# A selective scan over PSUM in two pieces instead of three, with TensorE's and ScalarE's orders rewritten around it

## The reference, cut to what matters

```
h  = softmax(x x^T / 16) x                      # within each segment of 128 rows
xz = layernorm(h) W_in^T ;  x_in, z = split(xz) # 2 x 512 wide
u  = silu(conv4(x_in) + b) ;  dt = softplus(u W_dt^T + b_dt)
B, C = u W_B^T, u W_C^T                         # 16 states
h_t = exp(dt_t A) h_(t-1) + dt_t B_t u_t        # for each of 512 channels x 16 states
y_t = sum over states of h_t C_t ;  h += (y silu(z)) W_out^T
h  += 64 experts, 8 chosen of 4 groups, capacity 256, on layernorm(h)
```

## Time and profile before

| | us |
|---|---|
| median of three runs | 3821.16 |
| lowest and highest | 3820.72, 3831.04 |
| the profiled execution, its own time | 3815.21 |
| its span, first to last instruction | 3813.3 |

### The profile page before, as it was taken

One profiled execution on the slowest core, in us unless ns is written; L12 is line 12 of the kernel. 1 busy time (PEld: TensorE's weight loads), 2 busy tenths in 40 slices (PEclk: granted clock), 3 DMA queues, 4 the chain that ended last, 5 costly groups with the idle time before them and its releaser, 6 DMA issues. The chain is left out here.

```text
span 3813.3 us, 65702 instructions
## 1 busy us (share of the span) xinstructions
PE 3190.2 (84%) x19681; PEld 2528.9 (66%) x19681; DVE 3016.4 (79%) x5267; ACT 2879.0 (75%) x5580; POOL 2106.1 (55%) x780
## 2 busy tenths in 40 slices
PE   5898898988888888888888898898898888566664
PEld 3777776776777677777777777676677667445453
DVE  3888888888888888888888888888888898544442
ACT  4998988888888888888888888888888888121110
POOL 0555555555555555555555555555555556157776
PEclk8999999999999999999999999999999998678887
DMA  2111111111111111111111111111111111157775
GB/s 84 47 47 55 55 43 56 57 57 55 51 53 40 56 57 57 57 57 52 54 57 57 57 55 43 57 57 57 49 56 52 40 52 50 42 135 146 147 151 86
DMA packets 175733, 241.57 MB, mean 63 GB/s; under 512 B 32816, under 2 KB 154128, under 8 KB 175376
## 3 DMA queue, kind: packets, MB, share of 16 engines
q1 hardware_dynamic: 150800, 199.44, 16.3%
q0 software_dynamic: 24576, 37.77, 6.0%
HBM read 176.07 MB, written 61.08 MB: 62 GB/s over the span
## 5 line engine op out<-in xcount | busy, mean ns | idle before, releaser
L345 POOL TENSOR_TENSOR hid<-hid,c_all 128x1536 f32<-128x1536 f32 x512 | 1771.0, 3459 | 1491.6 <-DVEq L563 1489.6
L568 DVE TENSOR_TENSOR_SCAN hid<-decay,hid,psB 128x512 f32<-128x512 f32 x1024 | 1310.7, 1280 | 119.3 <-PE psB L826 12.4
L826 PE MATMUL psB<-ident,dbu_t 128*128 128x128 f32 x6144 | 936.7, 285 | 236.8 <-DVE hid L568 224.0
L363 ACT ACTIVATE dbu_t<-dtu_t,b_t 128x512 f32<-128x512 f32 x1536 | 995.5, 714 | 159.8 <-PE psB L826 158.2
L375 ACT ACTIVATE decay<-dt,a_neg 128x383 f32<-128x383 f32 x2048 | 1085.8, 606 | 0.0
L826 PEld LDWEIGHTS psB<-ident,dbu_t 128*128 128x128 f32 x6144 | 721.8, 145 | 446.6 <-DVE hid L568 325.7
L838 PE MATMUL psY<-ident,hid 128*128 128x128 f32 x6144 | 780.7, 278 | 33.1 <-POOL hid L345 32.3
L838 PEld LDWEIGHTS psY<-ident,hid 128*128 128x128 f32 x6144 | 714.2, 145 | 77.6 <-POOL hid L345 34.4
L568 DVE TENSOR_TENSOR_SCAN hid<-decay,psB 128x512 f32<-128x512 f32 x512 | 624.0, 1219 | 103.4 <-PE psB L826 72.0
L898 PE MATMUL psM<-u,w_dt 128*128 128x384 f32 x1024 | 354.7, 489 | 18.3 <-ACT turned L384 14.7
L898 PEld LDWEIGHTS psM<-u,w_dt 128*128 128x128 f32 x1024 | 184.4, 190 | 127.8 <-ACT turned L384 21.3
(11 more groups left out here) (148 smaller groups left out, 3520.4 us busy)
## 6 DMA issues: line engine op xcount, KB each, us to landing
c_all<-bc_rows_dram SPq DMA_DIRECT2D x128, 768.0 KB, 4.9
out_dram<-h SPq DMA_DIRECT2D x64, 384.0 KB, 3.5
h<-out_dram SPq DMA_DIRECT2D x32, 384.0 KB, 3.4
x_weights_dram<-normed SPq DMA_DIRECT2D x32, 384.0 KB, 2.5
xs<-in_x_dram SPq DMA_DIRECT2D x32, 256.0 KB
e_wg<-in_gate_dram SPq DMA_DIRECT2D x64, 128.0 KB
e_wu<-in_up_dram SPq DMA_DIRECT2D x64, 128.0 KB
e_wd<-in_down_dram SPq DMA_DIRECT2D x64, 128.0 KB
```

Of the source, the lines that this page charges most:

```text
L345: nc.gpsimd.tensor_tensor(hid[k % 4][:, :, :], hid[k % 4][:, :, :], c_all[:, k, :].unsqueeze(1).to_broadcast([P, CH, L]), ALU.mult).then_i ...
L363: last = nc.scalar.activation(dbu_t[k % 2][:, t, :], dtu_t[q][:, t, :], ACT.Copy, scale=b_t[q][:, t, k:k + 1])
L568: nc.vector.tensor_tensor_scan(h[:, lo:hi], flat(decay[k % 4])[:, lo:hi], psB[:, j, :], h[:, lo - 1:lo] if j else 0.0, ALU.mult, ALU.add). ...
L826: last = nc.tensor.transpose(psB[:, j, i * P:(i + 1) * P], dbu_t[k % 2][:, t, c * P:(c + 1) * P], ident[:, :])
```

## The change

The scan of a step is made in two pieces, of 1024 and of 512 columns; `psB` still has three banks, and `turn_dbu` fills two banks (eight transposes) and then one (four). In TensorE's step `turn_dbu` 0 comes first, then `sum_y`, then `turn_dbu` 1, and all the step's products stand behind it. In ScalarE's step `first_rstd` comes first (that of sequence b-2 in step 1, no longer 2), then `scaled_dbu`, then all copies, with `softplus` among them, and `decays` nearly last. On VectorE both `drive`s are in step 11, behind `attended`; three waits of the routing move from behind their instruction to the head of the function that needs it. The transposed rows DU0 and DU1 are both made in step 12.

```diff
-PB = 3
+PIECES = ((0, 2), (2, 3))
+PB = len(PIECES)
...
-        psB = ps("psB", [P, PB, 512])
+        psB = ps("psB", [P, NSEG, 512])
...
@@ ScalarE's body
-                    if front:
-                        if k == 0:
-                            copy_turned("XN0", b, 0)
-                        if k in (1, 2):
-                            copy_xin(b, 2 * k - 2)
-                        if k in (5, 6, 7, 8):
-                            biased_dt(b, k - 5)
-                        if k in (12, 13):
-                            copy_dtu(b, r, 2 * (k - 12))
-                    if late and k == 9:
-                        copy_turned("X2T1", b, 1)
-
+                    if late and k == 1:
+                        first_rstd(o, 1)
+                    if early and k == 13:
+                        first_rstd(a, 0)
                     if of:
                         scaled_dbu(*of)
                     if front:
                         if k == 0:
+                            copy_turned("XN0", b, 0)
                             copy_turned("XN1", b, 1)
                         if k in (1, 2):
+                            copy_xin(b, 2 * k - 2)
                             copy_xin(b, 2 * k - 1)
...
+                        if k in (5, 6, 7, 8):
+                            biased_dt(b, k - 5)
+                        if k == 8:
+                            softplus(n, b, 1)
+                        if k == 12:
+                            copy_dtu(b, r, 0)
+                            copy_dtu(b, r, 1)
+                        if k == 13:
+                            copy_dtu(b, r, 2)
+                    if late and k == 9:
+                        copy_turned("X2T1", b, 1)
...
                     if late and k == 7:
                         copy_turned("X2T0", b, 0)
+                    if front and k == 7:
+                        softplus(n, b, 0)
                     if early and k == 8:
                         copy_prob_t(b)
-                    if front:
-                        if k == 9:
-                            copy_bc(n, b, r)
-                        if k == 12:
-                            copy_dtu(b, r, 1)
+                    if front and k == 9:
+                        copy_bc(n, b, r)
...
                     if of:
                         decays(*of)
-                    if late and k == 2:
-                        first_rstd(o, 1)
-                    if front:
-                        if k == 3:
-                            after(act, s_yz, n - 1)
-                            silu_z(b, r, 0)
-                            silu_z(b, r, 1)
-                        if k in (7, 8):
-                            softplus(n, b, k - 7)
-                    if early and k == 13:
-                        first_rstd(a, 0)
+                    if front and k == 3:
+                        after(act, s_yz, n - 1)
+                        silu_z(b, r, 0)
+                        silu_z(b, r, 1)
...
@@ VectorE
-                lo, hi = 512 * j, 512 * (j + 1)
+                lo, hi = 512 * PIECES[j][0], 512 * PIECES[j][1]
                 h = flat(hid[k % 4])
-                nc.vector.tensor_tensor_scan(h[:, lo:hi], flat(decay[k % 4])[:, lo:hi], psB[:, j, :],
+                nc.vector.tensor_tensor_scan(h[:, lo:hi], flat(decay[k % 4])[:, lo:hi], flat(psB)[:, lo:hi],
                                              h[:, lo - 1:lo] if j else 0.0, ALU.mult, ALU.add).then_inc(s_h, 1)
...
-                def step(ins, carried=False):
+                def step(ins, last=False):
                     done[0] += 1
                     ins.then_inc(s_rt, 1)
-                    dve.wait_ge(s_rt, ROUTE_STEPS * m + done[0])
-                    if carried:
-                        dve.sem_inc(s_turn, 1)
+                    if not last:
+                        dve.wait_ge(s_rt, ROUTE_STEPS * m + done[0])
...
-                step(nc.vector.tensor_tensor(flat(gsum), v[0], v[3], ALU.add), carried=True)
+                step(nc.vector.tensor_tensor(flat(gsum), v[0], v[3], ALU.add), last=True)
...
             def route_experts(m, step, done):
 
+                dve.wait_ge(s_rt, ROUTE_STEPS * m + done[0])
+                dve.sem_inc(s_turn, 1)
...
-                step(last, carried=True)
+                step(last, last=True)
...
             def weigh(m):
 
+                dve.wait_ge(s_rt, ROUTE_STEPS * (m + 1))
+                dve.sem_inc(s_turn, 1)
...
-                        if k in (10, 11):
-                            drive(n, b, r, k - 10)
+                    if early and k == 11:
+                        attended(a, b)
+                    if front and k == 11:
+                        drive(n, b, r, 0)
+                        drive(n, b, r, 1)
                     if early:
-                        if k == 11:
-                            attended(a, b)
...
@@ TensorE
-                for i in range(4):
-                    c, t = divmod(4 * j + i, NSEG)
-                    last = nc.tensor.transpose(psB[:, j, i * P:(i + 1) * P], dbu_t[k % 2][:, t, c * P:(c + 1) * P],
-                                               ident[:, :])
+                for i in range(4 * PIECES[j][0], 4 * PIECES[j][1]):
+                    c, t = divmod(i, NSEG)
+                    last = nc.tensor.transpose(flat(psB)[:, i * P:(i + 1) * P],
+                                               dbu_t[k % 2][:, t, c * P:(c + 1) * P], ident[:, :])
...
                 for k in range(NS):
+                    if scans:
+                        turn_dbu(b, k, 0)
                     if scans and k >= 3:
                         sum_y(b, k - 3)
                     if back and k < 3:
                         sum_y(m, k + NS - 3)
                     if scans:
-                        turn_dbu(b, k, 0)
                         turn_dbu(b, k, 1)
...
-                    if scans:
-                        turn_dbu(b, k, 2)
-
```

More of the change, by code:

```diff
@@ L718, in route_experts @@
                 step(last)
-                step(nc.vector.memset(gtop[:, :, TOPG:G], ABSENT), carried=True)
+                step(nc.vector.memset(gtop[:, :, TOPG:G], ABSENT))
+                dve.sem_inc(s_turn, 1)
                 for s in range(NSEG):
@@ L726, in route_experts @@
                     out=by_group(masked), in0=flat(gleft).unsqueeze(2).to_broadcast([P, NSEG * G, GE]), scalar=FAR,
-                    in1=by_group(biased), op0=ALU.mult, op1=ALU.add), carried=True)
+                    in1=by_group(biased), op0=ALU.mult, op1=ALU.add))
+                dve.sem_inc(s_turn, 1)
                 for s in range(NSEG):
                     last = nc.vector.max(top8[:, s, :], masked[:, s, :])
-                step(last, carried=True)
+                step(last, last=True)
                 assert done[0] == ROUTE_STEPS
             def weigh(m):
+                dve.wait_ge(s_rt, ROUTE_STEPS * (m + 1))
+                dve.sem_inc(s_turn, 1)
                 for s in range(NSEG):
@@ L964, in body @@
                             turn_normed("XN", b, 0, normed1)
+                            turn_normed("XN", b, 1, normed1)
                         if k in (1, 2):
                             project_xin(b, 2 * k - 2)
+                            project_xin(b, 2 * k - 1)
                         if k == 3:
                             project_z(b, 0)
-                        if k in (5, 6, 7, 8):
-                            project_dt(n, b, k - 5)
-                        if k in (12, 13):
-                            turn_dtu(n, b, 2 * (k - 12))
-                    if late and k == 9:
-                        turn_normed("X2T", b, 1, normed2)
-                    if early and k == 10:
-                        attend(b, 0)
-                    if back and k == 14:
-                        project_out(b, 0)
-                    if scans:
-                        turn_dbu(b, k, 2)
-                    if front:
-                        if k == 0:
-                            turn_normed("XN", b, 1, normed1)
-                        if k in (1, 2):
-                            project_xin(b, 2 * k - 1)
-                        if k == 3:
                             project_z(b, 1)
@@ L991, in body @@
                             project_z(b, 2)
+                        if k in (5, 6, 7, 8):
+                            project_dt(n, b, k - 5)
                     if early:
@@ L998, in body @@
                             scores(b)
-                    if late and k == 7:
-                        pe.wait_ge(s_xn[1], o + 1)
-                        turn_normed("X2T", b, 0, normed2)
-                    if early:
                         if k == 8:
@@ L1005, in body @@
                             turn("PT", b, [prob[:, s, :] for s in range(NSEG)])
-                    if front and k == 9:
-                        project_bc(b)
-                    if early and k == 10:
-                        attend(b, 1)
+                        if k == 10:
+                            attend(b, 0)
```

(23 more changed lines are left out.)

4 lines of the change are left out of this document (2 added, 2 removed).

## The result

| | before | changed |
|---|---|---|
| median of eight runs, us | 3818.11 | 3832.53 |
| lowest and highest | 3814.03, 3831.04 | 3827.13, 3841.73 |
| the profiled execution | 3815.21 | 3831.40 |
| its span | 3813.3 | 3829.2 |
| granted clock, mean | 0.940 | 0.937 |

The ratio is 1.0035, with a 95% interval of 1.002 to 1.0049: the changed kernel is slower, by about 13 us. That lies inside the range of the prediction (3770 to 3870) and 11 us above its point, but it is a change where none was forecast. All times here are of executions in the faster of the device's two states; one of the ten of e7_three took 8946 us, where the other nine took 3809 to 3820, and is left out.

The account below looks back on a forecast made before the run. VectorE was taken to bound most steps, TensorE steps 4 to 10, ScalarE's late instructions before step 14. (-1.04 + 1.25 for the clock) x 30 blocks gave +6, the last blocks -6: forecast 3821 us, range 3770 to 3870.

Parts of the forecast that it names:

- The cost of one scan: VectorE's scan in each step: large piece 2.29 us, fixed cost 0.15, whole scan 3.60, which is 0.31 less.
- T0 to T4: From the first scan piece's start in step 0 to that in step 4: -0.26 us per block, including +1.33 gate wait.
- T4 to T10: From scan start in step 4 to that in step 10, TensorE the chain: 37.4 against 36.92 us, +0.48 per block.
- T10 to T0: From scan start in step 10 to the next block's step 0: -0.95 us up to step 15, then -0.31.
- T15 to T0: From scan start in step 15 to that in the next block's step 0: -0.31 us per block.
- T13 to T15: From scan start in step 13 to that in step 15: 11.52 us, set by TensorE's O0, O1 and transposes.
- The clock: TensorE's clock falling ahead of the gate (about 1.5 us) and step 12 (about 1.0), half the blocks: +1.25 per block.
- The ends: The last two blocks, having little beside their scans, were to give back about 6 us.
- All four: Rival forecasts: clock holds, 3784 us (0.30); slower clock, 3859 (0.20); scan's fixed cost stays, 3868 (0.07); VectorE's whole gain, about 3510 (0.05).
- Rival 2: Clock falls in nearly every block ahead of the gate and of step 12: slower, 3859 us, chance 0.20.
- Rival 4: VectorE's whole gain arrives, 9.6 us per block: about 3510 us, chance 0.05.
- no change: Main forecast for the whole kernel: 3821 us, within 0.3% (11 us) of the kernel before, chance 0.38.

Follow-up runs that it names:

- e7_three: Changed kernel with the scan in three pieces of one bank each, keeping the new orders: 3814.7 us, ratio 0.9982.
- e1_gate: Changed kernel with the sum ahead of turn_dbu 0 in step 2 alone: 3770.4 us, ratio 0.9873.
- f1_smallfirst: Changed kernel with the small scan piece first (512 columns, then 1024): 3755.4 us, ratio 0.9833.
- e3_probt: Changed kernel with ScalarE's copy of PT ahead of softplus 1 again: 3804.8 us, ratio 0.9961.
- e4_rstd: Kernel before with first_rstd at the head of ScalarE's steps 1 and 13, nothing else changed: 3797.6 us, ratio 0.9942.
- e8_filler: Changed kernel with twelve unread transposes in TensorE's idle time ahead of turn_dbu 0 of step 2: 3840.3 us, ratio 1.006.
- e2_pieces: Kernel before with the scan in two pieces and nothing else changed: 3785.1 us, ratio 0.9914.
- g1_spread: Kernel before with the scan in two pieces, plus CB's wide products cut and laid between its narrow ones: 3759.4 us, ratio 0.9854.
- f2_small_probt: Changed kernel with 512 columns first, then 1024, and ScalarE's copy of PT ahead of softplus 1: 3710.3 us, ratio 0.9714.

## Why the prediction was right or wrong

**The cost of one scan: right.** 2285 ns was measured for 1024 columns against 2.29 us, and from 1219 at 512 that is 2.08 ns per column and 0.15 fixed. The Trainium skill ("DVE: opcode table, instruction layouts, handler registers and perf-mode slots", section 6, Feedback) says that the built-in scan runs at half throughput. The trace agrees: 2.08 ns per column against the 1.02 per element that the prediction found for ordinary operations.

**T0 to T4: right in mechanism and size.** The gate waits for the sum behind the large piece; 4.90 against 4.93. e1_gate and f1_smallfirst remove the cause in two different ways, and both times the wait is gone. The wait behind `gsum` was worth about 0.3: T0 to T1 went from 8.53 to 7.90, of which 0.31 are the scan's.

**T4 to T10: right, slightly small.** Where the clock holds it is 37.5 against the 37.4 of the forecast. The two causes named were both there: D2 late by 1.8, and CB's wait for PT, of which e3_probt gave back 1.0.

**T10 to T0: right.** The wait for `rs` is gone, O0 and O1 take its place. T15 to T0 fell by 0.19 in blocks without the jump, where 0.31 was forecast. T13 to T15 is 11.29 where the clock holds, against 11.52 worked out, and e4_rstd shows the same limit in the old order (11.08).

**The clock: right in kind, wrong in its shares.** Half the blocks were taken at both places. It was 16 of 26 ahead of the gate, at 1.4 us each on the mean (0.87 per block, 0.75 taken), and 6 of 26 ahead of or in step 12, at 1.1 (0.26, 0.5 taken). At a third place nothing was taken: behind CB, 8 of 26 blocks have a slow T9 to T10 where the kernel before had 4. The mean T4 to T10 is 0.45 over its shortest, where it was 0.24: +0.2 us per block, 5 us in all. At the two places that were named the clock cost 1.13 us per block, a little less than the 1.25 taken. That the idle time is what costs the clock ahead of the gate is shown by e8_filler. The step that failed here is "The clock", which priced falls at two places only: the trace of before already had T9 to T10 at 9.98 in three blocks instead of 8.33, and I did not ask what made them so. On the rule of the Trainium skill ("TensorE: Matmul & The Clock Gate", section "HAM oscillation — how this bites in real kernels"), that only idle gaps longer than these harm, the trace disagrees: 2.47 us of idle time were followed by the half level.

**The ends: wrong, and this is the larger miss.** The step "the last two blocks, which have little beside their scans, give back about 6" has the wrong sign. The last block's T1 to T2, with nothing to do but gate and scan, went from 5.80 to 8.89, as GpSimd's starts show:

```profile
3205.63 3.44 POOL L349 TENSOR_TENSOR hid<-hid,c_all 128x1536 f32<-128x1536 f32 x1 [4.24 <-DVEq L561]
3214.52 3.44 POOL L349 TENSOR_TENSOR hid<-hid,c_all 128x1536 f32<-128x1536 f32 x1 [5.45 <-DVEq L561]
```

```profile
3212.53 1.89 DVE L576 TENSOR_TENSOR yz_t<-psY,zs_t 128x512 f32<-128x512 f32 x3 [3.30 <-PE psY L842]
```

The gate waits there 3.3 us, at the half level, and nothing hides it; the last two blocks together take 3.6 us more, not 6 less. Adding up the two profiled executions: the 26 blocks +10.1, the blocks ahead of them +3.8 and behind them +2.7, the first scan 4.4 later, the rest of the program 5.1 less: +15.9 us, the difference of the spans. The sum of the prediction, +6 and -6, was right for the middle to 5 us and left out 11 at the ends, where I took the scan's gain and forgot that the gate's wait is there too. A second term was put at nothing, the start. Ahead of the first scan the changed order puts both `drive`s behind `attended`, and the transposes DU wait for them:

```profile
79.23 2.46 PE L851 MATMUL psM<-ident,u 128*128 128x128 f32 x12 [3.15 <-DVE u L672]
```

They begin at 74.63 in the kernel before. The first start of GpSimd is at 84.5 to 87.2 us in the four kernels with the old place of `drive` (before, e2_pieces, e4_rstd, g1_spread) and at 88.8 to 93.0 in the ten with the new one; no edit moved the `drive`s alone. The 5.1 us less at the other end are probably not the change's: e2_pieces and e4_rstd, whose edits are small, have 5.3 and 4.7 less there too.

**The rivals.** All four fell. Rival 2 (slower by the clock, 3859) has the right sign for the wrong reason: it was said to decide above some 55% of the blocks, and 62% fell ahead of the gate, but only 23% at its other place, and the two together cost less than the forecast had taken. What made the kernel slower than the forecast is the third place and the ends. Rival 4's sum comes to about 3527 with the 30 blocks of the others, not 3510, which changes nothing. The forecast of "no change" was a balance of a gain and a loss of nearly equal size, each of which could be off by more than the 11 us of the band.

**Where the expected gain went.** VectorE has 103 us less to do. The order of TensorE gave most of it back: a wait for two thirds of the scan at the head of each step, with the sum behind it. Undoing that in one step of sixteen gives 62 us, splitting the banks the other way 77.

## What to carry to other kernels

When two pieces of work are merged, ask what waits for the first of them, and what stands behind that waiting instruction in its queue; the small piece first keeps the merge's gain and frees the buffer early. Put an instruction that can run at once ahead of one that must wait, step by step, and not by one order for all: here the sum belongs first in the steps where TensorE waits, the transposes in those where TensorE is late. A forecast that is the difference of two equal terms is worth little until each is priced in the first and last blocks too.

## What the runs showed of the hardware that was not expected

TensorE's granted clock falls to the half level not only after idle time. In e2_pieces it fell in 19 of 26 blocks behind the 24 matmuls of 16 columns that the trace shows for CB, with the engine busy for five whole microseconds up to the fall in the block shown; each fall cost 1.66 us. With wide products laid between them (g1_spread) it fell in none. Idle time does it too: ahead of the gate 2.2 to 2.5 us of it were followed by the half level in 16 of 26 blocks, and with the time filled, in none of 14 (e8_filler). Stretches of some 16 us of nothing but 128-column transposes, as ahead of 1658.33 in the earlier trace rows, kept the full level in all 26 blocks of the kernel before, with idle time of up to 1.36 us among them.

The share of slow T9 to T10 is not set by the work of that stretch alone: it goes from none of 26 (f2_small_probt) to 19 in kernels that have the same narrow products there, and within one kernel blocks with the same work differ. An edit elsewhere can so cost 0.5 us per block in a stretch that it does not touch (e4_rstd). What sets the share was not settled; that it is how the block lies in time is a guess.
